# Attention pass over the edges: four heads scaled on each of two engines, one-hots made two items at a time, a longer one-hot ring

## The reference

```
for h in range(8):
    Wx = x @ Ws[h] + Wb[h]                      # 3125 x 64
    s = Wx[v_tgt] @ a_w[h, :64] + Wx[v_src] @ a_w[h, 64:] + a_b[h]
    s = leaky_relu(s, 0.2)
    alpha = segment_softmax(s, v_tgt, n)
    outs.append(segment_sum(alpha[:, None] * Wx[v_src], v_tgt, n))
```

## Time and profile before

| what | value |
|---|---|
| median of 3 runs | 2432.34 us (2432.03 to 2433.61) |
| profiled execution, span from first to last instruction | 2427.9 us |
| PE busy, share of the span | 2033.5 us, 84% |
| DVE busy | 1467.7 us, 60% |
| ACT busy | 919.9 us, 38% |
| POOL busy | 1037.0 us, 43% |
| pass over the edges, from the first gather to the last add | 149.6 to 768.2 us |

### The profile page before, as it was taken

The page is one execution under the profiler, slowest core; times in us unless marked ns, Lnnn a source line. Parts: engine busy times, 40 slices in busy tenths (PEclk is TensorE's granted clock), DMA queues, the critical chain, the costliest instruction groups (busy, mean ns, idle before and its releaser), DMA issues. The chain is left out here.

```text
span 2427.9 us, 33639 instructions
## 1 busy us (share of the span) xinstructions
PE 2033.5 (84%) x8826; PEld 1296.0 (53%) x8826; DVE 1467.7 (60%) x3150; ACT 919.9 (38%) x2800; POOL 1037.0 (43%) x1073
## 2 busy tenths in 40 slices
PE   5957888888885726089999998998999999999998
PEld 4735666666664224033333333455445888888534
DVE  6647999999998661565555555587763222222343
ACT  2324565566663503455555555444101111111000
POOL 1147777777752305177777777400001111111331
PEclk9978999999997858589999999998899999999999
DMA  4558888888863535777777777775314999999652
GB/s 142 127 175 241 248 248 248 245 248 248 248 189 114 213 103 114 242 241 224 223 224 224 223 224 238 237 269 186 119 63 163 367 365 366 366 365 362 235 192 88
DMA packets 278021, 543.48 MB, mean 224 GB/s; under 512 B 44001, under 2 KB 122049, under 8 KB 277677
## 3 DMA queue, kind: packets, MB, share of 16 engines
q0 software_dynamic: 82592, 268.48, 37.9%
q1 hardware_dynamic: 177219, 240.65, 29.2%
q10 hardware_dynamic: 18058, 32.64, 3.9%
HBM read 455.87 MB, written 86.57 MB: 223 GB/s over the span
## 5 line engine op out<-in xcount | busy, mean ns | idle before, releaser
L895 PE MATMUL g_psA<-g_G,g_oh 128*128 128x261 f32 x1760 | 447.5, 401 | 88.8 <-DVE acc L1062 69.8
L832 POOL DMA_INDIRECT g_G<-tab,src_of_item x440 | 430.6, 979 | 171.8 <-issue 104.5
L1186 PE MATMUL g_psA<-g_G,g_oh 128*128 128x512 f32 x832 | 395.9, 610 | 96.7 <-DMA g_G<-tab,src_of_tile 64.8
L1139 POOL DMA_INDIRECT g_G<-tab,src_of_tile x416 | 393.5, 946 | 171.0 <-issue 78.9
L1225 DVE TENSOR_TENSOR acc<-acc,g_psA 128x512 f32 x416 | 285.6, 687 | 214.1 <-PE g_psA L1186 175.2
L895 PEld LDWEIGHTS g_psA<-g_G,g_oh 128*128 128x128 f32 x1760 | 328.4, 195 | 157.0 <-issue 91.9
L953 ACT ACTIVATE g_G<-g_G 128x64 f32<-128x64 f32 x1320 | 320.2, 335 | 0.0
L1186 PEld LDWEIGHTS g_psA<-g_G,g_oh 128*128 128x128 f32 x832 | 147.1, 191 | 323.3 <-issue 203.7
L2360 PE MATMUL mo_bank<-mo_xT,mo_w 128*128 128x128 f32 x2304 | 269.1, 275 | 0.2 <-ACT mo_xT L2397 0.2
L2360 PEld LDWEIGHTS mo_bank<-mo_xT,mo_w 128*128 128x128 f32 x2304 | 263.0, 192 | 1.0 <-ACT mo_xT L2397 0.5
L2263 POOL DMA_INDIRECT mo_g<-tab,mo_slot x72 | 68.0, 945 | 457.1 <-PE mo_bank L2350 325.1
(11 more groups left out here) (420 smaller groups left out, 2554.7 us busy)
## 6 DMA issues: line engine op xcount, KB each, us to landing
mo_w<-in_L_ffn_w SPq DMA_DIRECT2D x216, 512.0 KB, 8.0
ys<-mo_y ACTq DMA_DIRECT2D x72, 256.0 KB, 5.7
g_ot<-reld SPq DMA_DIRECT2D x26, 512.0 KB, 6.1
ys<-sg_zeros SPq DMA_DIRECT2D x24, 512.0 KB, 3.9
g_G<-tab,src_of_item POOLq DMA_INDIRECT x440
g_pen<-pend SPq DMA_DIRECT2D x208, 32.0 KB
g_G<-tab,src_of_tile POOLq DMA_INDIRECT x416, 3.7
tab<-fi_row SPq DMA_DIRECT2D x25, 261.0 KB, 2.6
```

The lines of the kernel that those rows point to most:

```text
L832: q.indirect_dma_start(G[:, j % RING, :], None, tab0, bass.IndirectOffsetOnAxis(K.src[:, j:j + 1], 0)).then_inc(gs[g % 3], 16)
L895: ins = tens.matmul(psA[u][:, f, 0:HW], oh[:, n % OR, h, :], G[:, r + h, f * HW:(f + 1) * HW], start=(h == 0), stop=(h == SUP - 1))
L1139: g.indirect_dma_start(G[:, n % MR, :], None, table, bass.IndirectOffsetOnAxis(K.src1[:, n:n + 1], 0)).then_inc(got[n % MR], 16)
L1186: tens.matmul(psA[n % MB][:], oh[:, n % MO, :], G[:, n % MR, :], start=True, stop=True).then_inc(summed, 1)
```

## The change

The change alters three things in `phase_gat`. `HA` goes from 3 to 4, so that VectorE scales four heads of a row and ScalarE four. The one-hots of two neighbouring items are made by one instruction of twice the size, ahead of the scaling of the even one. The ring of one-hots `OR` goes from four items to six, and the wait on it is moved to fit.

```diff
-OR = 4
-HA = 3
+OR = 6
+HA = 4
...
             def prep(n):
                 r = n * SUP % RING
-                wait(v, summed, n - OR + 1)
-                vv.tensor_tensor(oh[:, n % OR], K.iota[:].unsqueeze(1).to_broadcast([P, SUP, P]),
-                                 K.rel[:, n * SUP:(n + 1) * SUP].unsqueeze(2).to_broadcast([P, SUP, P]), ALU.is_equal)
+                if n % 2 == 0:
+                    wait(v, summed, n - OR + 2)
+                    vv.tensor_tensor(oh[:, n % OR:n % OR + 2].rearrange("p i h t -> p (i h) t"),
+                                     K.iota[:].unsqueeze(1).to_broadcast([P, 2 * SUP, P]),
+                                     K.rel[:, n * SUP:(n + 2) * SUP].unsqueeze(2).to_broadcast([P, 2 * SUP, P]), ALU.is_equal)
```

## The result

The changed kernel is slower: 2450.29 us in the median of 4 runs (2448.78 to 2456.97), against 2432.19 for the kernel before (2428.55 to 2433.61). The ratio is 1.0078, with a 95% interval of 1.0053 to 1.0103. The forecast was 2443, in a range of 2431 to 2460. The profiled execution has a span of 2449.0 us, 21.1 more than before.

The account below looks back on a forecast made before the run. The prediction took a path through VectorE's early steps, then ScalarE's scaling ahead of i7, to bound each group. Adding +4.2 and clock +7, together +11, to the 2427.9 span gave 2439; with 4.4 for the median, 2443, range 2431 to 2460.

Parts of the forecast that it names:

- the two terms it named: ScalarE's scaling ahead of item i7, +4.2 us over 22 groups, and more falls of TensorE's clock, +7 us.
- VectorE's prices: Start to start on VectorE, 0.60 us for a scaling of 512 and 0.60 for a one-hot of 512.
- The wait at L1007: VectorE's carries L1007 would wait for TensorE's L863, a new idle time of about 0.5 us in each group.
- the step of i3: VectorE's odd step loses 0.46 us; nearly all becomes a wait for TensorE, and the path is 0.04 later.
- The link through ScalarE: Item i7 waits for ScalarE's eighth scaling and starts at 326.61 in place of 326.42, +0.19 us a group.
- the clock: TensorE's clock falls to half behind the stand ahead of i4 in 9 of 24 groups, before 2: +7 us.
- My +4.2 for the full clock: Groups without a fall of TensorE's clock grow by 0.19 us each, 22 x 0.19 = +4.2 us.
- No measurable change: Rival, chance 0.25: the clock falls no more often than now; within 0.2%, 4.9 us.
- The clock falls in nearly every group: Rival, chance 0.12: TensorE's longer stand ahead of i4 brings +24 to +30 us, 2456 to 2462.
- VectorE sets the pace: Rival, chance 0.10: VectorE's saved 1.3 us a group counts and the kernel gets faster, 2421 to 2430.
- Its cap: In the faster rival, GpSimd's gathers limit the gain to at most 0.5 us a group, 11 us.

Follow-up runs that it names:

- e5: The changed kernel with TensorE's turn of the weights (L876) moved from ahead of i6 to ahead of i5: 2451.50 us, ratio 1.0076 to the kernel before.
- e1: The kernel before with only the fourth head moved to ScalarE, one-hots item by item in a ring of four: 2437.43 us, ratio 1.0022.
- e8: The kernel before with the fourth head on ScalarE, four idle TensorE matmuls ahead of i4 and the weights turned ahead of i5: 2419.19 us, ratio 0.9943.
- e9: The changed kernel with six idle TensorE matmuls ahead of i4 and the weights turned ahead of i5: 2422.25 us, ratio 0.9979 to the kernel before.
- e11: The kernel before with the fourth head on ScalarE, six idle TensorE matmuls ahead of i4 and the weights turned ahead of i5: 2421.34 us, ratio 0.9975.
- e10: The kernel before with the fourth head on ScalarE and the weights turned ahead of i5, no idle matmuls: 2421.55 us, ratio 0.9977.

## Why the prediction was right, and where its sizes were off

The prediction held: slower, by the two terms it named.

**VectorE's prices were right.** I took 0.60 us for the one-hot of 512 and 0.60 for the scaling; they are 0.61 and 0.58. The rule of the Trainium skill that the prediction weighed (VectorE: DVE Perf Modes, on the TRN2 errata) would have saved 0.156 us for each pair and given 0.66 - 0.156 = 0.50 for the start to start of the new one-hot; the trace has 0.61.

**The wait at L1007 was right.** From 220 to 720 us the changed kernel has 23 waits of L1007 for L863, 8.5 us in total, 0.37 each where I had about 0.5; in the group above it starts 6.25 us behind L982, and by my sum it was 6.32. So the step of i3 gains nothing for the path, as written.

**The link through ScalarE was right, its size half.** I had +0.19 us for a group; i7 starts 17.70 behind L982 in place of 17.60, +0.10. From i5 to i7 it is 652.60 - 648.04 = 4.56 us, and by my sum it was 326.61 - 322.05 = 4.56, so ScalarE's part was met. What was off lies ahead of i5, which starts 13.14 behind L982 where I had 13.23: the 0.11 us from TensorE to VectorE at L1007 is 0.04 in the group above (640.84 + 0.27 to 641.15), and the rest of the way to the add was a little shorter as well. The e5 group of 20.06 us shows the link by taking it away. The profile doesn't name ScalarE ahead of i7, as I had expected. And "two more heads" in the prediction is one head more, two scalings an item, as its figures have it.

**The term that was mis-sized is the clock.** I had 9 falls of 1.0 us, with 2 before, +7. The 22 groups have 14. A group with a fall is 22.01 - 20.74 = 1.27 us longer than one without, so the falls cost 14 x 1.27 = 17.8, and those before 21.84 + 21.30 - 2 x 20.55 = 2.0 (groups 11 and 12 by the starts of L982). That is +15.8, twice my term. The eight groups with the full clock are a mean of 20.74, 0.19 above the 20.55 of before, and 22 x 0.19 = +4.2. Together 20.0, and measured 19.9.

Both sizes inside that term were off, the number of falls and the price of one. For the price I took 1.63 less the 0.57 us that TensorE stood ahead of i5 anyway. But my own sum has i5 at 322.05 and TensorE free at 321.80, so only 0.25 of that stand is left in the changed kernel, and the price should have been about 1.4. Against undisturbed groups of 20.65 the trace gives 22.01 - 20.65 = 1.36. With that price my 7 falls more would have been some 10 us, and the rest of the miss is their number. For the number I had no sum, only the guess of a bit over a third of the groups; it was 14 of 22.

My +4.2 for the full clock was met by luck. The link gives 22 x 0.10 = +2.2. Four of the eight groups end 0.23 us late, which I did not foresee (last section), and that is some 1 us in all. The rest belongs to the falls, at 1.36 each: 2.2 + 1 + 14 x 1.36 - 2.0 = 20.2.

**The rivals.** "No measurable change" failed at the number of falls, and the link alone would have been +2.2. "The clock falls in nearly every group" is nearer to the truth than I gave it credit for, and e5, which is another kernel, is that case: 19 falls. "VectorE sets the pace" is refuted by e1, where VectorE is busy 21.6 us less and even the groups with the full clock take 20.6 us in place of 20.55. Its cap was right in kind: `scores` waits for gathers in e8, e9 and e11, and e8 gained 0.31 us a group, where I had at most 0.5.

## What to carry to other kernels

An engine that is 96% busy need not be the one whose time counts: follow one period from its start back to its start, and for each edit ask what the freed engine waits for next. Work taken off in one step and put into its neighbour can cost even if the sum shrinks, because it moves two starts of TensorE apart. Where TensorE stands for 2 us in each period, look at its granted clock before and after; a few idle matmuls in the stand cost nothing here and were worth 13 us to the changed kernel. And look for the cap before optimising further: here the gathers allow a mean of 20.3 to 20.4 us for a group in the kernels that wait for them without falls of the clock (e8, e9).

## What the runs showed of the hardware

The clock fell behind stands of equal length in some groups and not in others: 2.35 us ahead of i4 in the group above with a fall, 2.34 in the one without. With the kernel before, 2.14 us bore 20 groups of 22; with e1, about 2.0 us bore only 16, and with e10 only 12. So with stands like these the time depends on how the period lies, and one of two groups that differ by nothing else in the rows can be 1.3 us longer.

In four of the 22 groups of the changed kernel the add of i7 starts 0.57 us behind the end of the item, where it is 0.21 in the others, and L982 behind it is late by 0.23. The rows of such a group, VectorE in order of time:

```profile
330.87 0.70 DVE L1064 TENSOR_TENSOR acc<-acc,g_psA 128x522 f32 x1 [1.61 <-PE g_psA L895]
331.48 0.55 DVE L982 TENSOR_REDUCE g_z<-g_psD 128x128 f32<-128x384 f32 x1
```

Item i7 ended at 330.30 there. The trace has the delay between the wait and the register instruction ahead of the add. In the other groups VectorE stands 1.26 us at this place, and the 1.61 of the row holds the 0.36 of the delay, so a longer stand is not what sets it off. It is not the change's own either: the kernel before has it once, at 412.34, where the item ended at 411.78. What causes it I don't know, and no run here was made to tell. It costs some 1 us in all.

GpSimd's gathers are a pace of their own. At the median of 0.946 us with 0.307 between them, 16 would take 20.05, but a few in each group are longer, and the mean of 0.979 makes 20.57, no less than VectorE and TensorE took. In e8 to e11 the 22 groups, 352 gathers, took 447.4 to 449.8 us, 1.27 to 1.28 for one. In e8, e9 and e11 that is a wait for the gathers. In e10, where nothing waits for them, the falls of the clock come to the same length.
